# An attention step reordered: the scores last, and VectorE in place of a copy by DMA

## The chip, the cores and the metric

The kernel runs on one core of a Trainium2 chip. The metric is the device time of one execution in microseconds (us), lower is better.

## The reference

A decoder layer on x (32 x 128 tokens x 128): an attention block, a retention block against a context, and a top-1 mixture of experts, with a layer norm after each. The change touches the attention block alone. For each of the 32 batch entries the 128 tokens are cut in two segments of 64, and each projection (128 to 1024) is reshaped to 16 heads of 64 rows:

```python
q, k, v = proj(Wq), proj(Wk), proj(Wv)     # xs @ W, then reshape(Bx, n_seg, H, L, dh): 16 heads, L = dh = 64
def step(carry, qkv):                      # over the two segments
    sq = elu(qs) + 1
    mem = mem + einsum('bhsk,bhsv->bhkv', sq, vs)
    zc = zc + (elu(ks) + 1).sum(-2)
    att_dot = softmax(qs @ ks.T * scale) @ vs
    num = sq @ mem;  den = sq.sum(-1) * zc
    att = gate * (num / den) + (1 - gate) * att_dot
    out_seg = att.reshape(Bx, L, H * DV) @ Wo
```

The reshape runs over the flat data of 64 tokens x 1024 columns, so that a row of a head is one of a token's 16 chunks of 64, and four tokens make a head. That is why q and v have to be laid out again, by head, before the memory is formed.

## The kernel before

`attention_phase` handles one batch entry per step t (32 steps and one that drains). Each engine runs its own instruction stream (`step` under `@block.sync`, `gpsimd`, `tensor`, `scalar`, `vector`), and semaphores tie the streams. The order on each engine is written out by hand; work of three batch entries is in flight: t (projections, turned rows, scores), u = t - 1 (softmax, memory) and t - 2 or t - 3 (attention output). What a step does, by engine:

- **TensorE**: projects v (into `proj_bank`), k (into `turn_bank`) and, later, q (`proj_bank` again), three matmuls for each half, L372. Between k and q: the sum of elu(k)+1 for u (L454), the output projection of t - 3 (`output`, L359, into `proj_bank[1]`), and the attention product of t - 2 (`attend`, L351). After q: it turns the rows of q and k (`turn_qk`, L385) into four banks (`qk_bank` = `score_bank` + `turn_bank`); forms the memory of u (`remember`, L414) from `pos_qv`; turns two of the four groups of u's probabilities (`turn_ps`, L401); makes the scores of t (`score`, L423 a dummy matmul that waits, L427 the scores); and turns the other two groups of u.
- **ScalarE**: copies v to `qv_out` (L534), exponentials of the scores (L502), copies k to `qk_tok` (L544), relu and exp for elu(k) (L521, L526), half of `attT` (`evac_att`, L508), copies q to `qk_tok` (L561), the four turned banks to `qkT` with all 128 partitions (L567), relu and exp for elu(q), and the turned probabilities to `psT` (L579).
- **VectorE**: row sums and reciprocals of u's softmax (L667, L669), z (L679, L683), `cut_k` (L637), the residual of t - 3 (L616, L619), the other half of `attT` (`move_att`, L625), the sum of sq over `pos_qv` (L697, L699), `cut_q` (L645, finishes elu(q)+1 into `qv_out`) alternating with `evac_memory` (L657), then maximum and subtraction of t's scores (L713, L717), and the last two `evac_memory`.
- **GpSimd**: stages x, scales the probabilities (L304), sums elu(k)+1 (L313), scales sq (L317), and multiplies v by the gate into `lhs` (L326).
- **SyncE** issues all DMAs of a step on one queue: for u the load of `pos_qv` from DRAM (two DMAs, L253), as soon as the store of u's `qv_out` has landed; the store of z (L256) and its broadcast load (L261); the copy of k's turned rows from partitions 64 to 127 of `qkT` to `kT` at partitions 0 to 63 (L267), from SBUF to SBUF; and the store of t's `qv_out` (L269).

So elu(q)+1 and v of an entry take this way: `cut_q(1)` on VectorE, store to DRAM, load as `pos_qv` in the next step, then `sq_sum` on VectorE and `remember` on TensorE. `qv_out` has one buffer, `pos_qv` two, and k's rows reach the scores through the copy:

```python
sp.wait_ge(qkT_evac, 4 * t + 4)
sp.dma_start(kT[:, :, :], qkT[DK:, :, :]).then_inc(kT_loaded, 16)          # L267
```
```python
pe.wait_ge(kT_loaded, 16 * (t + 1))
pe.matmul(score_bank[0][:, 0:1], qkT[0:DK, 0:2 * J, :], kT[:, 0:1, 0], ...)  # L423
```

Of the kernel before, what the change touches and what calls it, by code (L numbers as in the profile page):

```python
# [13 lines left out]
P = 128  # L14
B = 32
# [128 lines left out]
def attention_phase(nc, consts, const, r_all, stats, x, Wq, Wk, Wv, Wo, betas, scratch_qv, scratch_z):  # L144
# [5 lines left out]
    with ExitStack() as ctx:  # L150
# [20 lines left out]
        qv_out = sb("qv_out", [P, C, 2 * DK])  # L171
# [4 lines left out]
        qkT = sb("qkT", [P, P, C])  # L176
        kT = sb("kT", [DK, P, C])
# [8 lines left out]
        pos_qv = [sb(f"pos_qv{i}", [P, H, 2 * DK]) for i in range(2)]  # L186
# [25 lines left out]
        qv_loaded = [sem(f"qv_loaded{i}") for i in range(2)]  # L212
        vg_ready = sem("vg_ready")
        turned, qkT_evac, kT_loaded = sem("turned"), sem("qkT_evac"), sem("kT_loaded")
# [5 lines left out]
        att_ready, att_evac, att_moved = sem("att_ready"), sem("att_evac"), sem("att_moved")  # L220
# [12 lines left out]
        def _(sp):  # L233
# [11 lines left out]
            def step(half, p, one, two):  # L245
                t = 2 * half + p
                u = t - 1
                q = 1 - p
                if two:
                    sp.wait_ge(stored_qv, 16 * t)  # L250
                    for n in range(SEG):
                        src = scratch_qv[bass.ds(t, 1), n * L:(n + 1) * L]
                        sp.dma_start(pos_qv[q][n * L:(n + 1) * L, :, :],  # L253
                                     src.rearrange("o (h j) c e -> (o j c) h e", j=J)).then_inc(qv_loaded[q], 16)
# [8 lines left out]
                if one:  # L263
                    if not is_step(t, 0):
                        sp.wait_ge(scored, 2 * t)
                    sp.wait_ge(qkT_evac, 4 * t + 4)
                    sp.dma_start(kT[:, :, :], qkT[DK:, :, :]).then_inc(kT_loaded, 16)  # L267
                    sp.wait_ge(sq_ready, 2 * t + 2)
                    sp.dma_start(scratch_qv[bass.ds(t + 1, 1)].rearrange("o p c e -> (o p) c e"), qv_out[:, :, :]).then_inc(stored_qv, 16)  # L269
# [4 lines left out]
        def _(pool):  # L274
# [16 lines left out]
            def step(half, p, one, two):  # L291
                t = 2 * half + p
                q = 1 - p
                u = t - 1
                if one:
                    stage_x(t + 1, 1 - p)
                if two:
                    for hh in range(2):

                        pool.wait_ge(row_inv, 2 * u + hh + 1)  # L300
                        if hh == 0 and not is_step(u, 0):
                            pool.wait_ge(ps_turned, 4 * u)
                        s = slice(8 * hh, 8 * hh + 8)
                        pool.tensor_tensor(ps[:, s, 0:DK], s_exp[:, s, :],  # L304
                                           row_rec[:, s].unsqueeze(2).to_broadcast([P, 8, L]), ALU.mult).then_inc(p_ready, 1)
                if one:
# [8 lines left out]
                if two:  # L315
                    pool.wait_ge(sq_inv, t)
                    pool.tensor_tensor(ps[:, :, DK:], pos_qv[q][:, :, 0:DK],  # L317
                                       sq_rec[:, :].unsqueeze(2).to_broadcast([P, H, DK]), ALU.mult).then_inc(sqn_ready, 1)

# [4 lines left out]
                    for n in range(SEG):  # L324
                        s = slice(n * L, (n + 1) * L)
                        pool.tensor_tensor(lhs[0:L, 1 - n, :, :], pos_qv[q][s, :, DK:], ungate[s, :, :], ALU.mult).then_inc(vg_ready, 1)  # L326
                        pool.wait_ge(vg_ready, 2 * u + n + 1)

# [3 lines left out]
        def _(pe):  # L332
# [22 lines left out]
            def output(w):  # L355
                pe.wait_ge(att_evac, w + 1)
                pe.wait_ge(att_moved, w + 1)
                for c in range(C // 2):
                    last = pe.matmul(proj_bank[1][:, 0:D], attT[:, c, :], w_o[:, c, :], start=(c == 0), stop=(c == C // 2 - 1))  # L359
                last.then_inc(out_ready, 1)  # L360

            def step(half, p, one, two):
                t = 2 * half + p
                u = t - 1
                q = 1 - p
                hq = half if p == 1 else half - 1
                three = not is_step(t, 0, 1)
                four = not is_step(t, 0, 1, 2)
# [7 lines left out]
                def turn_qk(f):  # L376
# [5 lines left out]
                    elif not is_step(t, 0):  # L382
                        pe.wait_ge(shifted, 2 * t - 1 + f)
# [4 lines left out]
                def turn_ps(f):  # L388
# [3 lines left out]
                    elif one:  # L392
                        pe.wait_ge(qkT_evac, 4 * t + f + 3)
# [10 lines left out]
                def remember(n):  # L404

                    if n == 0:
                        pe.wait_ge(qv_loaded[q], 32 * (hq + 1))
                        if not is_step(u, 0):
                            pe.wait_ge(att_evac, u)
                            pe.wait_ge(att_moved, u)  # L410
                    k = (P, L)[n]
                    for h in range(H):
                        odd, at = h % 2, (h // 2 % 4 * 2 + n) * DK
                        last = pe.matmul(mix[odd * DK:(odd + 1) * DK, h // 8, at:at + DK], pos_qv[q][0:k, h, 0:DK],  # L414
                                         pos_qv[q][0:k, h, DK:], start=True, stop=True)
                    last.then_inc(mem_ready, 1)

                def score(hh):

                    if hh == 0:  # L420
                        pe.wait_ge(qkT_evac, 4 * t + 4)
                        pe.wait_ge(kT_loaded, 16 * (t + 1))
                        pe.matmul(score_bank[0][:, 0:1], qkT[0:DK, 0:2 * J, :], kT[:, 0:1, 0], start=True, stop=True)  # L423
                    for i in range(8):
                        for n in range(SEG):
                            tok = n * L + J * (8 * hh + i)
                            last = pe.matmul(score_bank[hh][n * L:(n + 1) * L, i * L:(i + 1) * L],  # L427
                                             qkT[0:DK, tok:tok + J, :], kT[:, tok:tok + J, :], start=True, stop=True)
                    last.then_inc(scored, 1)

                if one:
# [9 lines left out]
                    for hh in range(2):  # L441
                        if is_step(t, 1):
                            pe.wait_ge(qkT_evac, hh + 3)
                        elif not is_step(t, 0):
                            pe.wait_ge(psT_evac, 4 * t - 5 + hh)
                        project(turn_bank, w_k, hh, k_proj)
                    pe.wait_ge(v_evac, t + 1)
                if two:
                    if is_step(t, 1):
                        pe.wait_ge(const_loaded, 16)  # L450
                    if not one:
                        pe.wait_ge(sq_ready, 2 * t)
                    pe.wait_ge(k_summed, 4 * t)
                    pe.matmul(proj_bank[0][0:SEG * H, 0:DK], cst("z_sum"), k_sum[:, :], start=True, stop=True).then_inc(zc_ready, 1)  # L454
                if four:
                    if is_step(t, 3):
                        pe.wait_ge(wo_loaded, 16)
                    output(t - 3)
# [3 lines left out]
                if one:  # L462
                    if is_step(t, 0):
                        pe.wait_ge(w_split, 6)
                    if two:
                        pe.wait_ge(z_rec, t)
                    project(proj_bank, w_q, 0, q_proj)
                    if four:
                        pe.wait_ge(res_ready, t - 2)
                    project(proj_bank, w_q, 1, q_proj)  # L470
                    for f in range(4):
                        turn_qk(f)
                if two:
                    remember(0)
                    remember(1)
                    turn_ps(0)
                    turn_ps(1)
                if one:
                    score(0)
                    score(1)  # L480
                if two:
                    turn_ps(2)
                    turn_ps(3)

            run_steps(pe, step, B, peeled=2)
            pe.wait_ge(res_ready, B - 2)
            output(B - 2)
# [6 lines left out]
        def _(act):  # L494
# [9 lines left out]
            def evac_att(w):  # L504

                act.wait_ge(att_ready, 4 * w + 4)
                for i in range(2):
# [3 lines left out]
            def step(half, p, one, two):  # L511
# [15 lines left out]

                if one:
                    for hh in range(2):
                        c, src = chunks(proj_bank, hh)  # L530
                        act.wait_ge(v_proj, 2 * t + hh + 1)
                        if hh == 0 and not is_step(t, 0):
                            act.wait_ge(stored_qv, 16 * t)
                        last = act.activation(qv_out[:, c, DK:], src, ACT.Copy)  # L534
# [20 lines left out]
                if three:  # L555
                    evac_att(t - 2)
                if one:
                    for hh in range(2):
                        c, src = chunks(proj_bank, hh)
                        act.wait_ge(q_proj, 2 * t + hh + 1)  # L560
                        act.activation(qk_tok[:, c, 0:DK], src, ACT.Copy).then_inc(q_evac, 1)  # L561
                    for f in range(4):
                        act.wait_ge(turned, 4 * t + f + 1)
                        if f == 0 and not is_step(t, 0):
                            act.wait_ge(scored, 2 * t)
                            act.wait_ge(kT_loaded, 16 * t)
                        act.activation(qkT[:, :, 4 * f:4 * f + 4], qk_bank[f][:, :].rearrange("p (c s) -> p s c", c=4), ACT.Copy).then_inc(qkT_evac, 1)  # L567
# [14 lines left out]
                if two:  # L582
                    evac_ps(0)
                    evac_ps(1)
                if one:
                    exp_scores(t, 0)
                if two:
                    evac_ps(2)
                    evac_ps(3)
# [895 lines left out]
```

## Time and profile before

| | |
|---|---|
| median of 3 runs | 1029.44 us (1025.58 to 1029.86) |
| the profiled execution's own time | 1023.68 us |
| its span, first to last instruction | 1021.9 us |
| busy, whole span | PE 77%, PEld 67%, DVE 61%, ACT 53%, POOL 50% |
| granted TensorE clock, mean | 0.851 |
| attention phase | from the start to 719.9 us |

PE is TensorE's matmuls, PEld its weight loads, DVE VectorE, ACT ScalarE, POOL GpSimd, SPq the queue of SyncE. PEclk is the granted clock, 1.00 for 2.4 GHz and 0.50 for 1.2 GHz. A row in order of time gives start, duration, engine, line and tiles of a run of equal instructions ("x6"), and in brackets how long the engine stood idle before it and what ended that. Matmuls are pipelined, so the time that a group takes is read from the start of the group to the start of the next.

### The profile page before, as it was taken

The page shows a single profiled execution, that of the slowest core. Times are in us where ns is not written, and L with a number is a line of the kernel's source. Part 1 is how long each engine was busy: PE and PEld are TensorE (multiplying, and loading weights), DVE is VectorE, ACT ScalarE, POOL GpSimd, SP SyncE. Part 2 cuts the span into 40 slices and gives each one's busy share as a digit, 9 for nine tenths or more (in the row PEclk, how much of TensorE's full clock was granted, in tenths as well). Part 3 has the DMA queues.
Part 4 walks back from the last instruction along what each step waited for, and adds up shares of the span by engine and source line. Part 5 has one row for each costly group of instructions (what it writes and reads, how often), then busy time and mean ns, then how long its engine had stood idle before and what let it go on. Part 6 is the DMA issues. An engine that isn't in the chain of part 4 may idle for free. (4 is left out here: it accounts for less than half of the span.)

```text
span 1021.9 us, 26750 instructions
## 1 busy us (share of the span) xinstructions
PE 791.6 (77%) x9501; PEld 683.3 (67%) x9502; DVE 619.2 (61%) x1217; ACT 542.7 (53%) x1119; POOL 515.4 (50%) x524
## 2 busy tenths in 40 slices
PE   5688898899988899889989899987599450099940
PEld 4577777787877778778778787877366450089940
DVE  4466666666766767666676676766588450034438
ACT  4656666656676566665676666672222110067730
POOL 2364546655565555565555645564334116546742
PEclk8788989988998989898898988998799655589985
DMA  6565655655655665565655656654118501140023
GB/s 211 133 179 137 146 135 144 144 165 144 144 144 144 165 150 138 144 144 165 156 132 144 149 161 149 138 146 123 49 32 232 64 1 44 52 107 31 31 74 111
DMA packets 115499, 127.71 MB, mean 125 GB/s; under 512 B 6913, under 2 KB 101409, under 8 KB 109329
## 3 DMA queue, kind: packets, MB, share of 16 engines
q1 hardware_dynamic: 112928, 122.17, 48.1%
q0 software_dynamic: 2544, 5.21, 1.5%
q8 instruction: 15, 0.25, 0.1%
q14 instruction: 12, 0.09, 0.0%
HBM read 67.42 MB, written 43.16 MB: 108 GB/s over the span
## 5 line engine op out<-in xcount | busy, mean ns | idle before, releaser
L304 POOL TENSOR_TENSOR ps<-s_exp,row_rec 128x512 f32<-128x512 f32 x64 | 66.7, 1045 | 202.5 <-DVE row_rec L669 202.5
L326 POOL TENSOR_TENSOR lhs<-pos_qv,ungate 64x1024 f32<-64x1024 f32 x64 | 150.6, 2353 | 2.5
L313 POOL TENSOR_TENSOR e_qk<-e_qk 128x512 f32<-128x512 f32 (+2 forms) x96 | 79.3, 826 | 90.0 <-DVE e_qk L637 85.0
L502 ACT ACTIVATE s_exp<-s_exp 128x512 f32<-128x512 f32 x64 | 40.2, 628 | 137.0 <-DVE s_exp L717 137.0
L645 DVE SCALAR_TENSOR_TENSOR qv_out<-bank,e_qk 128x512 f32<-128x512 f32 x64 | 44.2, 692 | 104.4 <-ACT e_qk L526 103.5
L401 PE MATMUL bank<-const,ps 128*128 128x128 f32 x512 | 94.1, 342 | 2.9 <-issue 2.5
L657 DVE TENSOR_TENSOR lhs<-mix,zg_all 64x512 f32<-64x512 f32 x128 | 88.3, 690 | 7.5 <-DMA zg_all<-scratch_z 3.6
L579 ACT ACTIVATE psT<-bank 128x512 f32<-128x512 f32 x128 | 72.4, 595 | 22.1 <-PE bank L401 21.8
L427 PE MATMUL bank<-kT,qkT 64*64 64x64 f32 x2048 | 83.0, 249 | 0.0
L372 PE MATMUL bank<-w_v,x_cur 128*128 128x512 f32 x192 | 77.7, 559 | 3.6 <-DVE w_v L603 3.6
L401 PEld LDWEIGHTS bank<-const,ps 128*128 128x128 f32 x512 | 74.3, 175 | 8.7 <-issue 3.0
L427 PEld LDWEIGHTS bank<-kT,qkT 64*64 64x64 f32 x2048 | 77.4, 161 | 0.5
L526 ACT ACTIVATE e_qk<-e_qk 128x512 f32<-128x512 f32 x128 | 75.8, 664 | 0.0
L713 DVE TENSOR_REDUCE s_max<-bank 128x8 f32<-128x512 f32 x64 | 44.1, 689 | 51.6 <-PE bank L427 51.6
L385 PEld LDWEIGHTS bank<-const,qk_tok 128*128 128x128 f32 x512 | 55.4, 141 | 28.7 <-issue 28.7
L385 PE MATMUL bank<-const,qk_tok 128*128 128x128 f32 x512 | 62.3, 274 | 15.5 <-issue 12.5
L414 PE MATMUL mix<-pos_qv 64*64 64x64 f32 (+1 forms) x2048 | 71.4, 223 | 1.6 <-DVE attT L625 1.6
L567 ACT ACTIVATE qkT<-bank 128x512 f32<-128x512 f32 x128 | 66.3, 602 | 8.8 <-PE bank L385 8.8
L414 PEld LDWEIGHTS mix<-pos_qv 64*64 64x64 f32 (+1 forms) x2048 | 64.8, 136 | 9.0 <-issue 5.1
L521 ACT ACTIVATE e_qk<-bank 128x512 f32<-128x512 f32 x128 | 70.8, 623 | 0.0
L359 PE MATMUL bank<-w_o,attT 128*128 128x128 f32 x512 | 67.0, 285 | 1.6 <-DVE attT L625 1.6
L351 PE MATMUL mix<-psT,lhs 128*64 128x64 f32 x2048 | 66.7, 224 | 0.5 <-POOL lhs L326 0.5
(210 smaller groups left out, 1684.8 us busy)
## 6 DMA issues: line engine op xcount, KB each, us to landing
scratch_qv<-qv_out SPq DMA_DIRECT2D x32, 1024.0 KB, 4.0
pos_qv<-scratch_qv SPq DMA_DIRECT2D x64, 512.0 KB, 6.2
kT<-qkT SPq DMA_DIRECT2D x32, 512.0 KB, 4.1
zg_all<-scratch_z SPq DMA_DIRECT2D x64, 256.0 KB, 3.8
sorted_x<-padding SPq DMA_DIRECT2D x1, 2515.5 KB, 20.7
r_all<-in_x_dram SPq DMA_DIRECT2D x4, 512.0 KB, 6.7
cx<-in_ctx_dram SPq DMA_DIRECT2D x8, 256.0 KB, 2.8
w<-in_L_ffn_W_dram SPq DMA_DIRECT2D x1, 2048.0 KB, 9.4
```

The costliest lines, as they stand in the source:

```text
L313: pool.tensor_tensor(dst, e_qk[:, 0:c, DK:], e_qk[:, c:2 * c, DK:], ALU.add).then_inc(k_summed, 1)
L326: pool.tensor_tensor(lhs[0:L, 1 - n, :, :], pos_qv[q][s, :, DK:], ungate[s, :, :], ALU.mult).then_inc(vg_ready, 1)
L359: last = pe.matmul(proj_bank[1][:, 0:D], attT[:, c, :], w_o[:, c, :], start=(c == 0), stop=(c == C // 2 - 1))
L372: last = pe.matmul(bank[hh][:, :], x_cur[p][:, a, :], w[:, b, hh * BANK:(hh + 1) * BANK], start=(i == 0), stop=(i == 2))
L385: last = pe.transpose(qk_bank[f][:, i * P:(i + 1) * P], qk_tok[:, 4 * f + i, :], cst("ident"))
L401: last = pe.transpose(turn_bank[f % 2][:, i * P:(i + 1) * P], ps[:, 4 * f + i, :], cst("ident"))
L414: last = pe.matmul(mix[odd * DK:(odd + 1) * DK, h // 8, at:at + DK], pos_qv[q][0:k, h, 0:DK], pos_qv[q][0:k, h, DK:], start=True, stop=True)
L427: last = pe.matmul(score_bank[hh][n * L:(n + 1) * L, i * L:(i + 1) * L], qkT[0:DK, tok:tok + J, :], kT[:, tok:tok + J, :], start=True, sto ...
L521: act.activation(e_qk[:, c, slot * DK:(slot + 1) * DK], src, ACT.Relu, scale=-1.0).then_inc(done, 1)
L526: act.activation(e, e, ACT.Exp, scale=-1.0).then_inc(done, 1)
L579: act.activation(psT[:, 4 * f:4 * f + 4, :], turn_bank[f % 2][:, :].rearrange("p (h s) -> p h s", h=4), ACT.Copy).then_inc(psT_evac, 1)
L657: dve.tensor_tensor(dst, mix[odd * DK:(odd + 1) * DK, g, :].rearrange("p (i n k) -> p i n k", n=SEG, i=4), zg_all[odd * DK:(odd + 1) * DK, ...
```

## The change

- `kT` is no longer filled by a DMA. ScalarE copies only partitions 0 to 63 of the turned banks (to `qT`), and VectorE copies partitions 64 to 127 of each to `kT` (four copies of 64x512).
- TensorE's order becomes: v, k and q projections together, the sum of elu(k)+1 (now in `score_bank[0]`), `attend(t-2)`, `turn_qk`, `remember`, `output(t-2)` (now in `score_bank[1]`, one step earlier), all four `turn_ps`, then the scores.
- ScalarE: all four parts of `attT`, after the copies of q; the first exponential of u at the head of the next step.
- VectorE: `sq_sum` moves ahead of `cut_k`; the `kT` copies come behind `cut_k`; then `evac_memory` and `cut_q` alternate, the residual, two more `evac_memory`, and maximum and subtraction last.
- `qv_out` gets two buffers and `pos_qv` has one; its load also waits for `remember` and the gate product of the step before.
- GpSimd scales sq ahead of the sum of elu(k)+1, and stages x last.

```diff
@@ SyncE
                 if two:
                     sp.wait_ge(stored_qv, 16 * t)
+                    if not is_step(u, 0):
+                        sp.wait_ge(mem_ready, 2 * u)
+                        sp.wait_ge(vg_ready, 2 * u)
...
                 if one:
-                    if not is_step(t, 0):
-                        sp.wait_ge(scored, 2 * t)
-                    sp.wait_ge(qkT_evac, 4 * t + 4)
-                    sp.dma_start(kT[:, :, :], qkT[DK:, :, :]).then_inc(kT_loaded, 16)
                     sp.wait_ge(sq_ready, 2 * t + 2)
@@ TensorE, turn_qk
                     elif not is_step(t, 0):
-                        pe.wait_ge(shifted, 2 * t - 1 + f)
+                        pe.wait_ge(*((z_rec, t), (shifted, 2 * t))[f])
@@ TensorE, step
                     pe.wait_ge(v_evac, t + 1)
+                    for hh in range(2):
+                        project(proj_bank, w_q, hh, q_proj)
                 if two:
...
-                    pe.matmul(proj_bank[0][0:SEG * H, 0:DK], cst("z_sum"), k_sum[:, :], start=True, stop=True).then_inc(zc_ready, 1)
-                if four:
...
-                    output(t - 3)
+                    pe.matmul(score_bank[0][0:SEG * H, 0:DK], cst("z_sum"), k_sum[:, :], start=True, stop=True).then_inc(zc_ready, 1)
                 if three:
                     attend(t - 2, 0)
                     attend(t - 2, 1)
                 if one:
...
                     for f in range(4):
                         turn_qk(f)
                 if two:
                     remember(0)
                     remember(1)
-                    turn_ps(0)
-                    turn_ps(1)
-                if one:
+                if three:
...
+                    output(t - 2)
+                if two:
+                    for f in range(4):
+                        turn_ps(f)
+                if one:
+                    if three:
+                        pe.wait_ge(res_ready, t - 1)
                     score(0)
                     score(1)
-                if two:
-                    turn_ps(2)
-                    turn_ps(3)
@@ VectorE, step
-                if one:
-                    cut_k(0)
-                if not is_step(t, 0, 1, 2):
-                    residual(t - 3)
-                if one:
-                    cut_k(1)
-                if not is_step(t, 0, 1):
-                    move_att(t - 2)
...
+                    dve.wait_ge(qv_loaded, 32 * t)
...
+                    dve.tensor_reduce(sq_sum[:, :], pos_qv[:, :, 0:DK], X, ALU.add).then_inc(sq_summed, 1)
                     dve.wait_ge(sq_summed, t)
                     dve.reciprocal(sq_rec[:, :], sq_sum[:, :]).then_inc(sq_inv, 1)
                 if one:
+                    cut_k(0)
+                    cut_k(1)
+                if one:
+                    for f in range(4):
+                        dve.wait_ge(turned, 4 * t + f + 1)
...
+                        dve.tensor_copy(kT[:, :, 4 * f:4 * f + 4], qk_bank[f][DK:, :].rearrange("p (c s) -> p s c", c=4)).then_inc(kT_evac, 1)
+                if two:
+                    evac_memory(0)
+                if one:
                     cut_q(0)
                 if two:
-                    evac_memory(0)
+                    evac_memory(1)
                 if one:
                     cut_q(1)
-                if two:
-                    evac_memory(1)
+                if not is_step(t, 0, 1):
+                    residual(t - 2)
+                if two:
+                    evac_memory(2)
+                    evac_memory(3)
```

## Rows read from the trace of the kernel before

**Rows 1.** Order of time, TensorE, the first and the last of 29 such rows

```profile
96.20 0.35 PE L423 MATMUL bank<-kT,qkT 64*128 64x1 f32 x2 [2.35 <-DMA kT<-qkT]
...
692.76 0.38 PE L423 MATMUL bank<-kT,qkT 64*128 64x1 f32 x2 [1.82 <-DMA kT<-qkT]
```

**Rows 2.** Order of time, TensorE, the step after 332.98: start us, us, what

```profile
332.98 0.38 PE L423 MATMUL bank<-kT,qkT 64*128 64x1 f32 x2 [1.81 <-DMA kT<-qkT]
333.29 2.08 PE L427 MATMUL bank<-kT,qkT 64*64 64x64 f32 x64
335.30 1.10 PE L401 MATMUL bank<-const,ps 128*128 128x128 f32 x8
336.16 1.63 PE L372 MATMUL bank<-w_v,x_cur 128*128 128x512 f32 x6
...
339.32 2.05 PE L359 MATMUL bank<-w_o,attT 128*128 128x128 f32 x16
341.31 2.08 PE L351 MATMUL mix<-psT,lhs 128*64 128x64 f32 x64
...
345.36 1.94 PE L385 MATMUL bank<-const,qk_tok 128*128 128x128 f32 x16 [0.38 <-issue]
347.22 2.23 PE L414 MATMUL mix<-pos_qv 128*64 128x64 f32 x64
349.38 1.09 PE L401 MATMUL bank<-const,ps 128*128 128x128 f32 x8
352.30 0.38 PE L423 MATMUL bank<-kT,qkT 64*128 64x1 f32 x2 [1.82 <-DMA kT<-qkT]
```

**Rows 3.** Three stretches, busy PE, PEld, DVE, ACT, POOL, PEclk, DMA share, GB/s

```profile
34.80:38.30 3.50, 3.50 (x65) 3.42 (x64) 1.38 (x2) 0.09 (x1) 0.00 (x0) 0.50 0.41 159
312.00:318.70 6.70, 6.70 (x48) 5.83 (x45) 5.04 (x8) 3.01 (x6) 1.41 (x2) 0.50 0.65 183
332.00:352.20 20.20, 17.11 (x262) 14.85 (x262) 15.22 (x26) 13.50 (x26) 12.36 (x11) 1.00 0.65 158
```

**Rows 4.** Order of time, TensorE, the scores in the first stretch of Rows 3

```profile
34.73 3.68 PE L427 MATMUL bank<-kT,qkT 64*64 64x64 f32 x64
```

**Rows 5.** Order of time, VectorE, the same step and the end before it

```profile
331.83 0.69 DVE L645 SCALAR_TENSOR_TENSOR qv_out<-bank,e_qk 128x512 f32<-128x512 f32 x1
...
337.26 1.41 DVE L657 TENSOR_TENSOR lhs<-mix,zg_all 64x512 f32<-64x512 f32 x2
...
343.69 1.40 DVE L625 COPY attT<-mix 64x512 f32<-64x512 f32 x2
345.12 1.22 DVE L697 TENSOR_REDUCE sq_sum<-pos_qv 128x16 f32<-128x1024 f32 x1
346.38 0.25 DVE L699 RECIPROCAL sq_rec<-sq_sum 128x16 f32<-128x16 f32 x1
```

**Rows 6.** Order of time, DMA issues of SyncE, the same step

```profile
332.71 0.35 SPq L269 DMA_DIRECT2D scratch_qv<-qv_out  x1
336.73 1.48 SPq L253 DMA_DIRECT2D pos_qv<-scratch_qv  x2
342.01 0.34 SPq L256 DMA_DIRECT2D scratch_z<-zg  x1
345.08 1.24 SPq L261 DMA_DIRECT2D zg_all<-scratch_z  x2
```

**Rows 7.** DMA issues, from 337.5 to 337.7 us: the last column is us to landing

```profile
pos_qv<-scratch_qv SPq DMA_DIRECT2D x1, 512.0 KB, 7.1
```

**Rows 8.** Order of time, ScalarE, the same step as Rows 2

```profile
337.43 1.09 ACT L534 ACTIVATE qv_out<-bank 128x512 f32<-128x512 f32 x2
...
343.44 1.20 ACT L508 ACTIVATE attT<-mix 64x512 f32<-64x512 f32 x2 [1.41 <-PE mix L351]
```

**Rows 9.** Order of time, GpSimd, the same step

```profile
348.72 4.78 POOL L326 TENSOR_TENSOR lhs<-pos_qv,ungate 64x1024 f32<-64x1024 f32 x2
```

**Rows 10.** DMA issues of the whole page, the broadcast load of z

```profile
zg_all<-scratch_z SPq DMA_DIRECT2D x64, 256.0 KB, 3.8
```

More of the change, by code:

```diff
@@ L170, in attention_phase @@
         e_qk = sb("e_qk", [P, C, 2 * DK])
-        qv_out = sb("qv_out", [P, C, 2 * DK])
+        qv_out = [sb(f"qv_out{i}", [P, C, 2 * DK]) for i in range(2)]
         k_sum = sb("k_sum", [P, DK])
@@ L185, in attention_phase @@
         psT = sb("psT", [P, H, P])
-        pos_qv = [sb(f"pos_qv{i}", [P, H, 2 * DK]) for i in range(2)]
+        pos_qv = sb("pos_qv", [P, H, 2 * DK])
         lhs = sb("lhs", [P, SEG, H, DK])
@@ L356, in output @@
                 pe.wait_ge(att_evac, w + 1)
-                pe.wait_ge(att_moved, w + 1)
                 for c in range(C // 2):
-                    last = pe.matmul(proj_bank[1][:, 0:D], attT[:, c, :], w_o[:, c, :], start=(c == 0), stop=(c == C // 2 - 1))
+                    last = pe.matmul(score_bank[1][:, 0:D], attT[:, c, :], w_o[:, c, :], start=(c == 0), stop=(c == C // 2 - 1))
                 last.then_inc(out_ready, 1)
@@ L413, in remember @@
                         odd, at = h % 2, (h // 2 % 4 * 2 + n) * DK
-                        last = pe.matmul(mix[odd * DK:(odd + 1) * DK, h // 8, at:at + DK], pos_qv[q][0:k, h, 0:DK],
-                                         pos_qv[q][0:k, h, DK:], start=True, stop=True)
+                        last = pe.matmul(mix[odd * DK:(odd + 1) * DK, h // 8, at:at + DK], pos_qv[0:k, h, 0:DK],
+                                         pos_qv[0:k, h, DK:], start=True, stop=True)
                     last.then_inc(mem_ready, 1)
@@ L506, in evac_att @@
                 act.wait_ge(att_ready, 4 * w + 4)
-                for i in range(2):
+                for i in range(4):
                     last = act.activation(*att_part(i), ACT.Copy)
@@ L531, in step @@
                         act.wait_ge(v_proj, 2 * t + hh + 1)
-                        if hh == 0 and not is_step(t, 0):
-                            act.wait_ge(stored_qv, 16 * t)
-                        last = act.activation(qv_out[:, c, DK:], src, ACT.Copy)
+                        if hh == 0 and not is_step(t, 0, 1):
+                            act.wait_ge(stored_qv, 16 * u)
+                        last = act.activation(qv_out[p][:, c, DK:], src, ACT.Copy)
                     last.then_inc(v_evac, 1)
@@ L619, in residual @@
                 dve.bn_stats(stats[:, bass.ds(b, 1), :].rearrange("p o d -> p (o d)"), rb)
-            def move_att(w):
-                dve.wait_ge(att_ready, 4 * w + 4)
-                for i in range(2, 4):
-                    last = dve.tensor_copy(*att_part(i))
-                last.then_inc(att_moved, 1)
             def step(half, p, one, two):
@@ L700, in step @@
                 if one:
-                    cut_q(0)
+                    cut_k(0)
+                    cut_k(1)
+                if one:
+                    for f in range(4):
+                        dve.wait_ge(turned, 4 * t + f + 1)
+                        if f == 0 and not is_step(t, 0):
+                            dve.wait_ge(scored, 2 * t)
+                        dve.tensor_copy(kT[:, :, 4 * f:4 * f + 4], qk_bank[f][DK:, :].rearrange("p (c s) -> p s c", c=4)).then_inc(kT_evac, 1)
                 if two:
@@ L704, in step @@
                 if one:
-                    cut_q(1)
+                    cut_q(0)
                 if two:
                     evac_memory(1)
+                if one:
+                    cut_q(1)
+                if not is_step(t, 0, 1):
+                    residual(t - 2)
+                if two:
+                    evac_memory(2)
+                    evac_memory(3)
                 if one:
```

103 lines of the change are left out of this document (38 added, 65 removed).

## The prediction

> **What bounds the kernel now.** First the time of a step. The waiting dummy matmul starts at 96.20 and at 692.76 us, 28 steps apart [rows 1]: 596.56 / 28 = 21.31 us a step. TensorE in order of time [rows 2] shows one step of 19.32 us in which nothing is missing but 1.82 us of waiting for the `kT` copy and 0.38 us ahead of `turn_qk`: the other 17.1 us are matmuls back to back. So TensorE and that wait bound a step. The remaining 21.31 - 19.32 = 2.0 us are the clock: in that step it is granted in full, 1.00 (2.4 GHz), while from 312.0 to 318.7, behind another wait of the same kind, it is 0.50 (1.2 GHz) with TensorE busy throughout [rows 3]. What the low level costs is read from the 64 score matmuls: 3.68 us there, 2.08 at the full one [rows 2, 4], a factor of 1.77.
>
> The other thing to see is the way of elu(q)+1. `cut_q(1)` ends at 331.83 + 0.69 = 332.52 [rows 5]; the store is issued at 332.71 and the load, which waits for it to land, at 336.73 [rows 6]; the second half of the load is issued 0.82 behind, at 337.55, and takes 7.1 us to land [rows 7], so at 344.65. That is 12.1 us from `cut_q(1)` to landed, and the consumer `sq_sum` starts at 345.12 [rows 5]: hidden today with 0.5 us to spare in the fastest kind of step and about 2 us on average.
>
> **The change, part by part.** Let T be the start of v's projection in step t.
>
> *Removed.* The `kT` DMA and its wait: 1.82 us, and with it perhaps the 2.0 us of low clock.
>
> *Added on VectorE.* Four copies of 64x512 from PSUM. Such copies take 0.70 each (two in 1.40), `evac_memory` also 0.70 [rows 5]: 4 x 0.72 = 2.9 us with the gaps. Bounds: nothing less than 0.70, since the size is the same; above, I set 1.0, for the turned reading order, which no VectorE row shows; that would be 1.1 us more a step, hidden as far as `remember` ends later still. I take 0.72, the row of the same shape. Removed there: two copies for `attT`, 1.4 us. ScalarE makes them instead, 2 more at 0.60, 1.2 us [rows 8]. Four ACT copies shrink from 128 to 64 partitions, which by the equal 0.60 of `attT` (64) and `qv_out` (128) changes nothing [rows 8].
>
> *TensorE's new order.* With the pieces of [rows 2] (start to start): v, k and the sum 3.16, q 1.66 (0.55 an op, three ops for each half), `attend` 2.0, `turn_qk` 1.86, `remember` 2.16, `output` 1.99, `turn_ps` 4 x 0.43, scores 2.3. That is the same 17 us. Without any load to wait for: ScalarE starts its chain at T + 0.6 (maximum and subtraction of the first score half stand ahead), exponential 0.6, v to grow 4.6 (337.43 to the idle time ahead of 343.44) [rows 8], q 1.1, `attT` 2.4: T + 9.4. `turn_qk` is done about then; `remember`, `output`, four `turn_ps` that each wait for the bank of the one before last (0.6 lost), and the scores follow: T + 18.3. So TensorE's and ScalarE's own chain closes at about 18.4 us.
>
> *The load.* Here the change bites. It is a loop from `cut_q(1)` of one step to `cut_q(1)` of the next, and every link is now in series on VectorE:
>
> - `cut_q(1)` to landed 12.1, and to the start of the waiter 0.1: 12.2
> - `sq_sum` and reciprocal: 1.5 [rows 5]
> - `cut_k` twice, now behind `sq_sum`: 1.44
> - four `kT` copies: 2.9
> - `evac_memory`, `cut_q(0)`, `evac_memory`, `cut_q(1)`: 4 x 0.72 - 0.03 = 2.85
> - sum: 20.9 us.
>
> Before, `cut_k` stood ahead of the load's wait, the `kT` copies did not exist, and one `evac_memory` less lay between: the loop was about 17 us and fitted under 19.3. The kernel now waits for the load in every step: landed comes at T + 9, while VectorE is done with z at about T + 6.3 (the sum of elu(k)+1 ends at T + 4.8, then its two small operations). Two buffers for `pos_qv` or one make no difference to it, as `remember` and the gate products of the step before (4.78 us on GpSimd, [rows 9]) end before the store lands, by about 1.7 us; if that cover went, it would be paid in full. The page "DMA: Bandwidth & Descriptors" of the Trainium skill (Rules for kernel authors) says to issue a DMA early and wait on it late; this change waits on it earlier. By that rule alone, too, the load comes to the surface; the trace before, with its 0.5 us of slack, agrees.
>
> *z.* Its store is issued at T + 6.4 while the load is in flight. In the trace it is issued at 342.01 and the broadcast follows at 345.08, just after the load has landed at 344.65 [rows 6]: it queues behind it. Then 1.24 for issuing and 3.8 to land [rows 6, 10]: landed about 5 us after the load, against 5.9 until the first `evac_memory` wants it. Hidden with 1 us; costed at nothing; uncovered it would cost what it is late.
>
> *The clock.* TensorE passes T + 7.8 with two of four `turn_qk` done and then has nothing until `cut_k(0)`, 2.3 us behind the landing: an idle stretch of some 3 us, longer than the 1.82 us after which the clock falls today. Then come one turn (0.43 more if slow) and `remember`, and the first `evac_memory` needs the latter. At full clock they end 2.8 us after `cut_k(1)`, level with the `kT` copies; wholly at the low level `remember` costs 2.16 x 0.77 = 1.65 more and the turn 0.45, together 2.1. So this term lies between 0 and 2.1. The trace has a step whose wait leaves the clock up and a stretch where it is low [rows 3], so it will not be all of it in each step; I take 1.3, some 60% of the bound, because the idle stretch is longer and stands right ahead. `output`, `turn_ps` and the scores may be slow as well; that eats the 2.5 us by which TensorE's own chain is ahead.
>
> **Sum.** A step of 20.9 + 1.3 = 22.2 us against 21.31: +0.89 x 31 = +27.6 us. At the drain the `attT` copies stand alone, twice 1.20 instead of side by side with VectorE: +1.2. The profiled execution took 1023.7 us (span 1021.9), so 1052 on its terms; the median of the runs shown is 1029.4, 5.8 above it, and the same sum on that is 1058 us. About 0.5% (5 us) is what a measurement of this kernel can tell from no change.
>
> **Rivals.**
>
> 1. *The loop bounds, but the clock stays up where it matters.* 20.9 a step: -0.41 x 31 + 1.2 = -11.5, or 1018. For it: low stretches do not follow every wait [rows 3]. Against: the idle stretch is longer than today's.
> 2. *TensorE stays the bound and only its gap closes.* The load would have to land by T + 6.3, 2.7 us sooner than the trace has it. Then 18.4 plus today's 2.0 of low clock, 20.4: -0.91 x 31 + 1.2 = -27, or 1002. For it: nothing waits for the load today. Against: the two transfers are the same ones, of the same size and on the same queue. The page "Perfetto Trace Analysis" of the Trainium skill (Identifying the Most-Contended Engine) would have one work on the engine with the highest occupancy and look for its gaps; by that rule this case is the one to expect.
> 3. *Slower by the clock.* The low level covers the turn and `remember` in every step: 20.9 + 2.1 = 23.0, +1.69 x 31 + 1.2 = +54, or 1083. It decides from the point where `remember` ends later than the `kT` copies. For it: the idle stretch comes right ahead of it in each step.
> 4. *Between 1 and the forecast*, near 21.3 a step: no change.
>
> That the change does not do what it says is no case here: the copy is gone and its four replacements stand in the stream.
>
> **How the numbers follow.** Forecast case (21.45 to 22.8 a step) 0.53, rival 1 0.17, rival 2 0.08, rival 3 0.12, rival 4 0.10. The range takes the forecast case, rival 4, rival 1 from somewhat below its centre, and of rival 3 the lower half: 1016 to 1080. The forecast case's own range is 1035 to 1077. Faster by over 0.5%: rival 2 and rival 1, 0.25. Within 0.5%: 0.10. Slower: 0.65.
>
> **What would show it.** In the profile of the changed kernel: `sq_sum` on VectorE waits for the DMA of `pos_qv` in every step, 2 to 3 us; `cut_q(1)` to `cut_q(1)` is 21 to 23 us and equals the step; TensorE idles some 3 us in the middle of `turn_qk` and not ahead of the scores; the low clock falls on `remember` and `output`; the four `kT` copies take 0.70 each. I am wrong if `sq_sum` does not wait, if the load lands in less than 12 us from `cut_q(1)`, or if `remember` runs at full clock.

## The result, and the profile after

| | before | after |
|---|---|---|
| median | 1027.51 us (4 runs) | 1050.70 us (4 runs, 1047.14 to 1052.50) |
| profiled execution: own time, span | 1023.68, 1021.9 us | 1051.29, 1049.5 us |

The ratio is 1.0222, with a 95% interval of 1.018 to 1.0264: the change makes the kernel 23 us slower. The forecast was 1058 us, with a range of 1016 to 1080.

The first thing to compare is the time of a step. `sq_sum` runs once in each of 32 steps, so the first and last start in its row (the view of one tile: count, duration min/median/max in ns, first and last start) give it. Before:

```profile
L697 DVE TENSOR_REDUCE sq_sum<-pos_qv x32: 1210/1220/1222, 46.6 to 705.0; 128x16 f32<-128x1024 f32 x32
```

After:

```profile
L665 DVE TENSOR_REDUCE sq_sum<-pos_qv x32: 1219/1220/1222, 46.0 to 727.4; 128x16 f32<-128x1024 f32 x32
```

That is 658.4 / 31 = 21.24 us a step before and 681.4 / 31 = 21.98 after: 31 x 0.74 = 23.0 us of the 27.6 by which the two spans differ. From the last `sq_sum` to the end of the attention phase it is 719.9 - 705.0 = 14.9 us before and 20.1 after. With the start, 0.6 us earlier, this accounts for the whole.

The waits of the kernel after, from 96 to 715 us (total, times, longest), in place of TensorE's wait for `kT`, which was 1.9 us a step (54.1 us in 29 waits):

```profile
PE bank L377 <- DVE e_qk L615: 73.7, 28, 4.5
DVE sq_sum L665 <- DMA pos_qv<-scratch_qv: 71.1, 28, 4.5
DVE lhs L633 <- PE mix L406: 40.1, 28, 2.9
```

VectorE waits for the load 2.5 us in each step, TensorE stands 2.6 us in the middle of its four turns until `cut_k` has run, and VectorE waits 1.4 us more for `remember`. One step in order of time, first TensorE, to be set beside [rows 2]:

```profile
330.61 2.08 PE L347 MATMUL mix<-psT,lhs 128*64 128x64 f32 x64
332.62 1.09 PE L377 MATMUL bank<-const,qk_tok 128*128 128x128 f32 x8
337.23 1.94 PE L377 MATMUL bank<-const,qk_tok 128*128 128x128 f32 x8 [3.52 <-DVE e_qk L615]
339.10 3.88 PE L406 MATMUL mix<-pos_qv 128*64 128x64 f32 x64
342.91 3.78 PE L354 MATMUL bank<-w_o,attT 128*128 128x128 f32 x16
346.48 1.14 PE L394 MATMUL bank<-const,ps 128*128 128x128 f32 x8
```

VectorE in the same step, beside [rows 5], from the last `cut_q` of the step before:

```profile
321.76 0.69 DVE L621 SCALAR_TENSOR_TENSOR qv_out<-bank,e_qk 128x512 f32<-128x512 f32 x1
...
335.02 1.22 DVE L665 TENSOR_REDUCE sq_sum<-pos_qv 128x16 f32<-128x1024 f32 x1 [3.42 <-DMA pos_qv<-scratch_qv]
336.28 0.25 DVE L667 RECIPROCAL sq_rec<-sq_sum 128x16 f32<-128x16 f32 x1
336.45 1.23 DVE L615 SCALAR_TENSOR_TENSOR e_qk<-bank,e_qk 128x512 f32<-128x512 f32 x2
337.71 2.52 DVE L676 COPY kT<-bank 64x512 f32<-64x512 f32 x4
343.12 0.69 DVE L633 TENSOR_TENSOR lhs<-mix,zg_all 64x512 f32<-64x512 f32 x1 [2.89 <-PE mix L406]
```

And the stages of this step (stretch, busy PE, PEld, DVE, ACT, POOL, PEclk, DMA share, GB/s), beside [rows 3]:

```profile
326.00:337.20 11.20, 7.71 (x97) 6.24 (x93) 6.53 (x13) 9.49 (x18) 2.64 (x3) 0.97 0.59 110
337.30:346.00 8.70, 8.70 (x86) 8.13 (x87) 5.66 (x9) 3.18 (x6) 8.31 (x7) 0.50 0.14 36
```

Here the whole loop can be read off. `cut_q(1)` ends at 321.76 + 0.69 = 322.45; the load has landed, and `sq_sum` starts, at 335.02, 12.6 us later. The idle stretch of 3.52 us falls behind two of the four turns, and right behind it the clock is at 0.50: `remember` takes 3.8 us from start to start instead of 2.16. The first `evac_memory` waits 2.89 us for it, and only behind that can the next `cut_q` run.

The steps are not all alike. The step before this one had `remember` at the full clock:

```profile
313.95 1.22 DVE L665 TENSOR_REDUCE sq_sum<-pos_qv 128x16 f32<-128x1024 f32 x1 [1.38 <-DMA pos_qv<-scratch_qv]
...
319.60 0.68 DVE L633 TENSOR_TENSOR lhs<-mix,zg_all 64x512 f32<-64x512 f32 x1 [0.43 <-PE mix L406]
...
357.92 1.22 DVE L665 TENSOR_REDUCE sq_sum<-pos_qv 128x16 f32<-128x1024 f32 x1 [1.09 <-DMA pos_qv<-scratch_qv]
```

From `sq_sum` to `sq_sum`, the step with the wait of 0.43 us took 335.02 - 313.95 = 21.07 us, and the one with the wait of 2.89 us took 357.92 - 335.02 = 22.90. Of the 27 steps whose `remember` starts between 96 and 690 us, 10 have it at the full clock.

### The profile page after: what moved, and what is told of

Its sections match the earlier page's. It is cut to its first block and busy times, and to the rows that moved or that the text cites. A ratio compares the mean times of both kernels' runs of the same rounds, so it can differ in the third digit from the quotient of the medians.

```text
span 1049.5 us, 26951 instructions
## 1 busy us (share of the span) xinstructions
PE 792.1 (75%) x9501; PEld 685.0 (65%) x9502; DVE 637.7 (61%) x1281; ACT 570.8 (54%) x1183; POOL 512.7 (49%) x524
## 5 line engine op out<-in xcount | busy, mean ns | idle before, releaser
L302 POOL TENSOR_TENSOR ps<-pos_qv,sq_rec 128x1024 f32<-128x1024 f32 x32 | 60.9, 1904 | 155.3 <-DVE sq_rec L667 155.3
L406 PE MATMUL mix<-pos_qv 64*64 64x64 f32 (+1 forms) x2048 | 95.5, 266 | 5.7 <-DMA pos_qv<-scratch_qv 5.7
L406 PEld LDWEIGHTS mix<-pos_qv 64*64 64x64 f32 (+1 forms) x2048 | 87.6, 176 | 15.9 <-issue 7.2
L560 ACT ACTIVATE qT<-bank 64x512 f32<-64x512 f32 x128 | 69.7, 587 | 43.0 <-PE bank L377 42.2
L665 DVE TENSOR_REDUCE sq_sum<-pos_qv 128x16 f32<-128x1024 f32 x32 | 39.0, 1220 | 84.8 <-DMA pos_qv<-scratch_qv 84.8
L354 PEld LDWEIGHTS bank<-w_o,attT 128*128 128x128 f32 x512 | 81.6, 250 | 5.4 <-issue 2.7
L676 DVE COPY kT<-bank 64x512 f32<-64x512 f32 x128 | 80.6, 692 | 1.0
L499 ACT ACTIVATE attT<-mix 64x512 f32<-64x512 f32 x128 | 75.7, 592 | 3.8 <-PE mix L347 2.6
L394 PE MATMUL bank<-const,ps 128*128 128x128 f32 x512 | 70.5, 281 | 9.1 <-ACT psT L572 9.1
L394 PEld LDWEIGHTS bank<-const,ps 128*128 128x128 f32 x512 | 58.5, 145 | 17.9 <-ACT psT L572 8.7
L419 PE MATMUL bank<-kT,qT 64*64 64x64 f32 x2048 | 69.0, 224 | 0.0
```

What stands on the lines that cost most here:

```text
L354: last = pe.matmul(score_bank[1][:, 0:D], attT[:, c, :], w_o[:, c, :], start=(c == 0), stop=(c == C // 2 - 1))
L394: last = pe.transpose(turn_bank[f % 2][:, i * P:(i + 1) * P], ps[:, 4 * f + i, :], cst("ident"))
L499: last = act.activation(*att_part(i), ACT.Copy)
L560: act.activation(qT[:, :, 4 * f:4 * f + 4], qk_bank[f][0:DK, :].rearrange("p (c s) -> p s c", c=4), ACT.Copy).then_inc(qT_evac, 1)
L676: dve.tensor_copy(kT[:, :, 4 * f:4 * f + 4], qk_bank[f][DK:, :].rearrange("p (c s) -> p s c", c=4)).then_inc(kT_evac, 1)
```

## The experiments

All times are medians, and ratios are to the kernel before on the same chip, with their 95% intervals. The changed kernel itself is at 1.0222 (1.018 to 1.0264). The theory is the load's loop. Its rivals are the single buffer of `pos_qv`, VectorE's added copies, and TensorE's new order. Diffs are cut where they show `...`.

**Two buffers for `pos_qv` again.**

```diff
-        pos_qv = sb("pos_qv", [P, H, 2 * DK])
+        pos_qv = [sb(f"pos_qv{i}", [P, H, 2 * DK]) for i in range(2)]
...
-                    if not is_step(u, 0):
-                        sp.wait_ge(mem_ready, 2 * u)
-                        sp.wait_ge(vg_ready, 2 * u)
```

> The changed kernel with two buffers for pos_qv again, and without the two waits of its load on the step before. Theory (the load's loop: cut_q(1), store, load, sq_sum, cut_k, kT copies, cut_q(1)): the load is held by the store's landing and not by its buffer, so nothing moves: 1047 to 1053 us. Rival (the single buffer holds the load back by the gate products on GpSimd): the load starts up to 1 us earlier in each of 31 steps, 1020 to 1035 us.

1044.26 us, ratio 1.0202 (1.0183 to 1.0222). That interval lies inside the one of the changed kernel, and the time is 3 us below the range of the theory and 9 us above the rival's: the buffer is not the cause. The profiled step of 21.83 us, against 21.98, leaves room for no more than about 0.15 us a step, and one single step of 24.8 us in the changed kernel's profile makes up 0.1 of that.

**`kT` by DMA again, the rest as changed.**

```diff
-                if one:
-                    for f in range(4):
...
-                        dve.tensor_copy(kT[:, :, 4 * f:4 * f + 4], ...).then_inc(kT_evac, 1)
...
+                    sp.wait_ge(qT_evac, 4 * t + 4)
+                    sp.dma_start(kT[:, :, :], qT[DK:, :, :]).then_inc(kT_evac, 16)
```

> The changed kernel with kT filled by the SBUF-to-SBUF DMA again, and no copies on VectorE; scores stay last, sq_sum stays ahead of cut_k. Theory: the four kT copies run beside the last turns and remember, on which the first evac_memory waits in any case (0.4 us at the full clock, 2.9 at the low one), so taking them away shortens the loop by nothing and the DMA is hidden by the scores' late place unless the copy's transfer meets the store: 1045 to 1058 us. Rival (the copies are what makes VectorE late): 2.6 us off each of 31 steps, 965 to 980 us.

ScalarE again copies all 128 partitions of the turned banks here. The result is 1046.26 us, ratio 1.0206 (1.017 to 1.0242): the same as with the copies. The 2.5 us of VectorE copies cost nothing here. What they occupied turns into waiting for `remember`. Waits of this run from 96 to 690 us:

```profile
DVE lhs L636 <- PE mix L410: 109.5, 26, 5.4
```

That is 4.2 us a step against 1.4 with the copies. So the replacement of the DMA by copies neither costs nor gains anything in the changed order.

**`sq_sum` behind `cut_k`, and behind the `kT` copies too.** On GpSimd the sum of elu(k)+1 goes ahead of the scaling of sq in both. The edits, in words:

```diff
 # first run                          # second run
+                cut_k(0), cut_k(1)   +                cut_k(0), cut_k(1)
                 sq_sum, sq_rec       +                kT copies
-                cut_k(0), cut_k(1)                    sq_sum, sq_rec
                 kT copies            -                cut_k(0), cut_k(1)
                                      -                kT copies
```

> The changed kernel with sq_sum and its reciprocal moved behind cut_k, ahead of the kT copies (and on GpSimd the sum of elu(k)+1 ahead of the scaling of sq). Theory: two cut_k, 1.25 us, leave the loop, and TensorE's four turns no longer wait for the load, so that remember starts as soon as the load lands: the loop is 12.3 + 1.5 + 2.6 + 2.8 = 19.2 us, plus up to 1 us of low clock, 31 steps of 21.98 - 19.2 to 20.2: 965 to 1000 us. Rival (TensorE's order and VectorE's added 2.6 us of copies bound, not the load): within 10 us of the changed kernel, 1040 to 1060.

> The changed kernel with sq_sum behind cut_k and also behind the kT copies (the same swap on GpSimd). Theory: the kT copies leave the loop too, which falls to some 17 us, under TensorE's and ScalarE's own chain of 18.4; sqn then comes 0.5 us late for the turned probabilities, so 18.5 to 20 us a step: 940 to 990 us, at or below the run with sq_sum between the two. Rival (VectorE's added copies or TensorE's order bound): 1040 to 1060.

998.63 us, ratio 0.9744 (0.9713 to 0.9775), and 998.85 us, 0.9746 (0.9726 to 0.9767). Both are 5% below the changed kernel. The first time lies in the theory's range, at the upper end, with a step of 636.2 / 31 = 20.5 us where the theory had 19.2 to 20.2; the second misses its 940 to 990 and gains nothing over the first (20.5 us a step as well). Its trace says what took over. In the rows below come VectorE, then SyncE's issues, then the landing of the store of z that is issued at 310.81:

```profile
314.99 1.22 DVE L674 TENSOR_REDUCE sq_sum<-pos_qv 128x16 f32<-128x1024 f32 x1
316.24 0.25 DVE L676 RECIPROCAL sq_rec<-sq_sum 128x16 f32<-128x16 f32 x1
319.99 0.68 DVE L633 TENSOR_TENSOR lhs<-mix,zg_all 64x512 f32<-64x512 f32 x1 [3.49 <-DMA zg_all<-scratch_z]
```
```profile
307.00 1.49 SPq L254 DMA_DIRECT2D pos_qv<-scratch_qv  x2
310.81 0.35 SPq L257 DMA_DIRECT2D scratch_z<-zg  x1
315.27 1.20 SPq L262 DMA_DIRECT2D zg_all<-scratch_z  x2
```
```profile
scratch_z<-zg SPq DMA_DIRECT2D x1, 8.0 KB, 4.3
```

An 8 KB store lands only after 4.3 us, at 315.1; the second half of the 1 MB load issued ahead of it on the same queue is in flight until about 314.9 (issued at 307.8, 7.1 us). The landing goes with the load in the changed kernel too: a store of z issued at 331.76 lands after 3.4 us, just behind the load, and one issued at 312.74, when the load is nearly done, after 1.4. The broadcast follows, and `evac_memory`, which stands ahead of `cut_q`, waits for it: 3.49 us in this step, 63.1 us in 29 waits in all. This is the z path that I had costed at nothing with 1 us of cover. The cover was `sq_sum`, `cut_k` and the copies in series behind the landing. The second order leaves only `sq_sum` of it; the first leaves out `cut_k`, and its waits for z come to 17.9 us in 15 steps.

**GpSimd's swap alone.** In words:

```diff
-                sqn: ps[:, :, DK:] <- pos_qv * sq_rec
                 sum of elu(k)+1
+                sqn: ps[:, :, DK:] <- pos_qv * sq_rec
```

> The changed kernel with only GpSimd's part of the two runs that moved sq_sum: the sum of elu(k)+1 ahead of the scaling of sq. Theory (the gain of those runs is that of sq_sum's place): the scaled sq is ready later, but still about when the first turn_ps wants it: 1042 to 1056 us. Rival (the swap gave the gain): 995 to 1020 us.

1028.91 us, ratio 1.0036 (1.0012 to 1.0059): neither what the theory said nor what the rival said, but 19 us below the changed kernel. If the two effects add, some 19 of the 49 us of the two runs above belong to the swap, and 30 to the place of `sq_sum`. TensorE in this run, one step:

```profile
324.09 2.08 PE L347 MATMUL mix<-psT,lhs 128*64 128x64 f32 x64
326.11 1.09 PE L377 MATMUL bank<-const,qk_tok 128*128 128x128 f32 x8
329.50 1.22 PE L377 MATMUL bank<-const,qk_tok 128*128 128x128 f32 x8 [2.29 <-DVE e_qk L615]
330.65 2.23 PE L406 MATMUL mix<-pos_qv 128*64 128x64 f32 x64
332.81 2.05 PE L354 MATMUL bank<-w_o,attT 128*128 128x128 f32 x16
335.26 1.09 PE L394 MATMUL bank<-const,ps 128*128 128x128 f32 x8 [0.40 <-POOL ps L311]
336.68 1.09 PE L394 MATMUL bank<-const,ps 128*128 128x128 f32 x8 [0.33 <-ACT psT L572]
337.70 0.38 PE L415 MATMUL bank<-kT,qT 64*128 64x1 f32 x2
338.00 2.08 PE L419 MATMUL bank<-kT,qT 64*64 64x64 f32 x64
340.47 1.65 PE L364 MATMUL bank<-w_v,x_cur 128*128 128x512 f32 x6 [0.38 <-POOL x_cur L281]
```

The swap adds two small waits of 0.4 us on GpSimd, ahead of `turn_ps` and of v's projection. TensorE's idle time in a step stays about what it was, but now it is in more pieces, and the piece ahead of `remember` is 2.2 us on average and 3.5 at most, instead of 2.6 and 4.5. The granted clock over 500 us goes from 0.90 to 0.95 (the seventh column; the changed kernel first, then the swap):

```profile
100.00:600.00 500.00, 431.62 (x5937) 375.78 (x5936) 338.63 (x591) 336.70 (x638) 266.22 (x226) 0.90 0.47 121
```
```profile
100.00:600.00 500.00, 429.42 (x6114) 369.90 (x6115) 348.23 (x608) 347.00 (x654) 276.20 (x234) 0.95 0.48 124
```

`remember` is then at the full clock in 18 of 27 steps instead of 10 of 27, and in such a step the time is the bare loop: 329.50 lies 20.91 us behind its like in the step before, at 308.59. That the clock rises with the swap is measured; that it does so because the idle time is divided is my reading, and no run here varies that alone.

**More work in the idle time.** To take the clock by itself, the second turn of q and k is made four times over, in the time in which TensorE waits anyway.

```diff
-                    for i in range(4):
+                    for i in range(4 * (4 if f == 1 else 1)):
+                        i %= 4
                         last = pe.transpose(qk_bank[f][:, i * P:(i + 1) * P], ...)
```

> The changed kernel with the second turn_qk of each step made four times over (twelve transposes more, 1.4 us of TensorE at the full clock, into the same bank with the same result, in the idle time in which it waits for the load). Theory (the idle time lowers the clock, and remember at the low clock lengthens the loop): with less idle time the clock stays up more often, the wait of the first evac_memory for remember falls from 1.4 us on average to under 1, and more work makes the kernel faster by 5 to 25 us: 1022 to 1043. Rival (the low clock does not depend on this idle time, or is hidden): equal, 1044 to 1050, or up to 15 us slower where the idle time was shorter than the added work.

1027.35 us, ratio 1.0028 (1.001 to 1.0046). Twelve transposes more in every step make the kernel 20 us faster. The clock over 100 to 600 us is 0.97, and the wait for `remember` falls from 1.4 to 0.8 us a step:

```profile
DVE lhs L634 <- PE mix L407: 22.8, 28, 2.2
```

Nothing else was added or moved, and the step falls from 21.98 to 21.26 us, of which 0.6 is the shorter wait for `remember`. That shows that the low clock on `remember` costs time, and that work in the gap gives some of it back. It does not show which idle time lowers the clock: TensorE still idles 1.7 us in the gap of a step here, at a clock of 0.97, while the kernel before idles 1.9 us ahead of its scores, at 0.90 over the same 500 us. What else decides stays open.

**`cut_q` ahead of `evac_memory`.**

```diff
+                if one:
+                    cut_q(0)
+                    cut_q(1)
                 if two:
                     evac_memory(0)
-                if one:
-                    cut_q(0)
-                if two:
                     evac_memory(1)
-                if one:
-                    cut_q(1)
```

In the changed kernel as it is:

> The changed kernel with both cut_q ahead of the first evac_memory; sq_sum stays ahead of cut_k. Theory (the loop holds remember only because evac_memory stands ahead of cut_q): the loop from cut_q(1) to cut_q(1) is then 12.3 to landed, 1.5, 1.25, and about 4 us of turns, copies of q and exponentials on ScalarE until the last cut_q: 19 to 20 us a step, free of remember at the low clock. Against the changed kernel 1.5 to 2.5 us off each of 31 steps: 965 to 1000 us. Rival (the wait of sq_sum itself, and TensorE's idle time in its turns, is what costs, wherever cut_q stands): 1030 to 1050 us.

985.07 us, ratio 0.9621 (0.9557 to 0.9684), and 620.8 / 31 = 20.0 us a step. VectorE behind its `kT` copies, one step:

```profile
307.34 2.52 DVE L676 COPY kT<-bank 64x512 f32<-64x512 f32 x4
310.45 1.29 DVE L621 SCALAR_TENSOR_TENSOR qv_out<-bank,e_qk 128x512 f32<-128x512 f32 x2 [0.60 <-ACT e_qk L517]
311.87 1.41 DVE L633 TENSOR_TENSOR lhs<-mix,zg_all 64x512 f32<-64x512 f32 x2
```

`remember` is out of the loop: VectorE's wait for it comes to 1.1 us in the whole stretch from 96 to 690 us, against 40.1 us in the changed kernel. It still waits 46.9 us for the load, in 26 steps.

Together with `sq_sum` behind the copies and GpSimd's swap:

> The changed kernel with sq_sum behind the kT copies (as in the run before) and also both cut_q ahead of the first evac_memory. Theory: no step of the load's way stands in front of cut_q any more but sq_sum, the store starts some 3 us earlier, the load lands before remember wants it, and the broadcast of z no longer queues behind the load, which took 2 to 3.5 us a step in the run with sq_sum behind the kT copies: the step is TensorE's and ScalarE's own chain of 18.3 to 19.3 us: 935 to 970 us. Rival (the z path bounds by itself): no faster than that run, 990 to 1000 us.

940.79 us, ratio 0.9216 (0.9169 to 0.9263). The wait for z's broadcast is gone (3.4 us in the whole stretch from 96 to 690 us, against 63.1 before this move), the clock is 1.00 from 100 to 600 us, and a step takes 575.4 / 31 = 18.6 us, close to the 18.4 at which the prediction put TensorE's and ScalarE's own chain. This run keeps TensorE's new order, so that order as such does not cost what the changed kernel loses.

In the kernel before, with its DMA copy:

> The kernel before with both cut_q ahead of the first evac_memory, its DMA copy for kT left. Theory (TensorE's wait for kT bounds there, the load's loop has slack): 0.7 us less in a loop that does not bind: 1018 to 1030 us. Rival (the loop binds there too, as in the run with VectorE's copies, where this move gave 31 us): 990 to 1010 us.

1023.28 us, ratio 0.9983 (0.997 to 0.9997): 0.2%, practically nothing. There the loop has slack, and the same move that is worth some 60 us in the changed kernel gains nothing to speak of.

**VectorE's copies in the kernel before.** Its order, its two buffers, and only the copy moved off the DMA.

```diff
-                    sp.dma_start(kT[:, :, :], qkT[DK:, :, :]).then_inc(kT_loaded, 16)
@@ VectorE, behind sq_sum
+                if one:
+                    for f in range(4):
+                        dve.wait_ge(turned, 4 * t + f + 1)
...
+                        dve.tensor_copy(kT[:, :, 4 * f:4 * f + 4], qk_bank[f][DK:, :]...)
```

> The kernel before, with its order and its two buffers, and only the kT copy moved from the DMA to four VectorE copies behind sq_sum. Theory: TensorE's wait of 1.82 us goes, and much of the 2 us of low clock with it, but the copies lengthen the load's loop from 16 to 18.7 us, so 18.7 to 19.7 a step instead of 21.3: 950 to 980 us. Rival (VectorE's copies cost as much as the wait they remove, or the scores' wait comes back as another): 1010 to 1030 us.

943.67 us, ratio 0.9233 (0.9197 to 0.9269): faster than the theory's range. Clock 1.00, 18.6 us a step, and VectorE waits for the load a little (0.7 us a step), which fits a loop of about 18.7 us. So in the order of the kernel before, the part of the change that its title names is worth 80 us; what the changed kernel loses, 107 us against this run, comes with the rest of the change, the new orders of the engines and the buffers. With both `cut_q` ahead of `evac_memory` as well:

> The kernel before with four VectorE copies for kT behind sq_sum, and both cut_q ahead of the first evac_memory. Theory: the loop shortens by 0.7 us and the z path hides as before; TensorE's 17.1 us of work are then nearly the bound: 18.0 to 19.2 a step, 930 to 965 us, at or below the run without the move of cut_q. Rival: VectorE, busy 17 us a step, delays the maxima of the scores, so that nothing is gained over that run.

912.22 us, ratio 0.8915 (0.8879 to 0.895), below the theory's 930 to 965 us. This is the best version, below both kernels. Its TensorE, one step:

```profile
300.85 0.38 PE L420 MATMUL bank<-kT,qkT 64*128 64x1 f32 x2
...
313.33 1.94 PE L381 MATMUL bank<-const,qk_tok 128*128 128x128 f32 x16 [0.37 <-issue]
315.20 2.23 PE L411 MATMUL mix<-pos_qv 128*64 128x64 f32 x64
...
318.50 0.38 PE L420 MATMUL bank<-kT,qkT 64*128 64x1 f32 x2
```

17.65 us from scores to scores, with 0.37 us idle: the 17.1 us of matmuls of [rows 2] and little else. The scores wait for nothing. The 1.82 us of waiting and the 2 us of low clock are both gone.

## Why the prediction was right, point by point

- *The load's loop bounds.* Right. The waiting row of `sq_sum` appears in all 28 steps, and the size of 20.9 us at full clock is met: 21.07 in the changed kernel's step from 313.95, 20.91 in the step of the swap. That it is met so closely is in part luck: `cut_k` twice took 1.26 instead of 1.44 and the copies 2.5 instead of 2.9, while `cut_q(1)` to `sq_sum` took 12.1 to 12.6 instead of 12.2 and `evac_memory` waited 0.4, which the sum did not have.
- *The loop of the kernel before, "about 17 us".* Its own terms give less: 12.2, 1.5 and three operations of 0.72 are 15.9. The conclusion, that it fitted, stands, and the run with `cut_q` moved in the kernel before bears it out.
- *The four copies as a link in series.* Nearly right in size, but not a link that counts alone: the run with the DMA shows that they run beside the turns and `remember`, which take the same time or more. I had seen the two level, but listed the copies as the link; without them the loop is as long.
- *One or two buffers make no difference.* Right.
- *z hidden with 1 us.* Right for this change. The cover is real, and its loss was seen in the run with `sq_sum` last, at 3.49 us in one step.
- *The clock: a term between 0 and 2.1, taken at 1.3.* The mechanism was right, and the run with more work shows it; the size is 21.98 - 20.9 = 1.1 on average. `remember` wholly at the low level delayed `evac_memory` by 2.89 - 0.43 = 2.5 us, but the step grew by less, from 21.07 to 22.90, since the way from `cut_q(1)` to the next `sq_sum` was 0.6 us shorter behind it. The bound held for the step. One sign of being wrong was named that did in part come true: `remember` runs at the full clock in about a third of the steps.
- *The drain: +1.2.* Mis-sized. It came to +5.2: `remember` (3.88 us) and both output projections (3.78 and 3.42) ran at or near the low clock there, behind waits of 5.69 and 2.58 us, where the kernel before had 2.23, 1.95 and 2.02. TensorE in the drain of the changed kernel:

```profile
727.42 3.88 PE L406 MATMUL mix<-pos_qv 128*64 128x64 f32 x64 [5.69 <-DMA pos_qv<-scratch_qv]
731.24 3.78 PE L354 MATMUL bank<-w_o,attT 128*128 128x128 f32 x16
...
743.11 3.42 PE L354 MATMUL bank<-w_o,attT 128*128 128x128 f32 x16 [2.58 <-ACT attT L499]
```

- *The sum.* 23.0 + 5.2 - 0.6 = 27.6 against the 28.8 forecast, on the profiled executions; the medians differ by 23.2. The closeness of 27.6 is luck: the steps gave 4.6 us less than forecast and the drain 4.0 more.
- *The rivals.* The loop with an undisturbed clock (1018) is what the added transposes and GpSimd's swap come near, 1027 and 1029. The step of 23.0 us that goes with 1083 occurs, but in only 4 of the 27 steps from 96 to 690 us is `remember` wholly at the low level. TensorE as the bound (1002) did not come. Moving the load's wait behind `cut_k`, or behind the copies too, together with the swap gives 49 us, of which some 30 are the wait's place. The page "DMA: Bandwidth & Descriptors" of the Trainium skill (Rules for kernel authors) says to issue a DMA early and wait on its semaphore late, and these runs agree.

## What to carry to other kernels

Write down the loop that closes over a step (last producer, store, landing, load, first consumer, and everything that stands in series on the consumer's engine before the next producer), and keep it below the busiest engine's own time. Whether a DMA is worth removing depends on the loop: the same replacement gained 80 us in the order of the kernel before and nothing in the changed order, where the place of one wait (some 30 us) or of one pair of instructions (some 60 us) decided. Try the parts of such a change one at a time: the DMA's replacement alone was the better kernel. Where TensorE must wait ahead of work that others wait for, look at the clock too: harmless work in the gap was worth 20 us here, and an order that divided the idle time 19.

## What the runs showed of the hardware that I had not expected

- This kernel got faster by doing more. 12 extra transposes a step raised the mean granted clock from 0.90 to 0.97 between 100 and 600 us and took 2% off the time of the changed kernel.
- With the idle time of a step mostly in three pieces (2.3, 0.4 and 0.4 us in the step shown) the granted clock was 0.95; with one main piece of 1.2 to 4.5 us, 0.90. In the stretch from 305 to 350 us it was 1.00 against 0.89. The kernel before, with pieces of 1.9 and 0.4 us, had 0.90 as well, so the length of the pieces alone does not explain it.
- An 8 KB store took 4.3 us to land with 1 MB of load ahead of it on its queue, and 1.4 us with that load nearly done; the load's second half took 7.1 us in the first case, as in the kernel before [rows 7].
- VectorE emptied one half of the partitions of four PSUM banks (316.64 to 319.16 us) while ScalarE emptied the other half (316.14 to 318.18), and neither was slower for it: VectorE's copies took 692 ns on average, as against 694 for copies of the same shape in the kernel before, and ScalarE's 587 against 602.
